# Third attention layer's finishing laid into the units of the expert mixture, with split weights streamed from DRAM

## The reference

```python
# L0_gnn, one layer (three in a row); y = attention over 100000 edges and the node itself
y = gat_conv(h, src, dst, w_l[i], a_s[i], a_d[i], b_l[i])
y = jax.nn.elu(y)
y = layer_norm(y, g_l[i], bt_l[i])
h = y + identity
...
x = x + _L0_gnn_ref(xn, ...) + _L0_mix_ref(xn[None], ...)[0]
x = x + _L0_ffn_ref(_layernorm(x, axis=-1)[None], ...)[0]

# L0_ffn: 8 experts, all computed for every node
w = jax.nn.softmax(feat @ Wr + br, axis=-1)
h = jax.nn.relu(_bn(jnp.einsum('bfd,edh->bfeh', x, W1) + b1, g1, be1, m1, v1))
h = jax.nn.relu(_bn(jnp.einsum('bfeh,ehk->bfek', h, W2) + b2, g2, be2, m2, v2))
y = jnp.einsum('bfeh,ehd->bfed', h, Wo) + bo
return jnp.einsum('bfed,fe->bfd', y, w)
```

## Time and profile before

| | us |
|---|---|
| median of 3 runs | 6968.39 |
| lowest, highest | 6960.25, 6972.53 |
| the profiled execution's own time | 6968.1 |
| its span in the trace | 6966.3 |
| busy in it: PE, DVE, ACT, POOL | 5315.0, 4790.6, 4135.7, 3522.9 |

### The profile page before, as it was taken

How to read it: one execution, slowest core, us unless ns; L and a number is a source line. 1 busy time by engine, 2 the same in 40 slices (tenths; PEclk the granted TensorE clock), 3 DMA queues, 4 the chain that set the end, 5 groups by cost and what they waited for, 6 DMA issues and landing times. The chain is left out here.

```text
span 6966.3 us, 97579 instructions
## 1 busy us (share of the span) xinstructions
PE 5315.0 (76%) x22260; PEld 3745.2 (54%) x22260; DVE 4790.6 (69%) x13210; ACT 4135.7 (59%) x13375; POOL 3522.9 (51%) x3571
## 2 busy tenths in 40 slices
PE   1768888745888886558888825999998887788698
PEld 1634444433555554535555514888884566565446
DVE  5756666684777777767777786666662487777693
ACT  4568989874989997669999862333335322111142
POOL 3377777727777773577777700000000477777501
PEclk8878888876999998779999867999998998788799
DMA  6344444434444443354444432000007534333402
GB/s 179 121 128 120 120 119 121 115 119 140 122 127 123 124 124 103 122 151 122 127 123 123 121 101 74 18 18 18 27 9 242 195 116 125 108 108 102 131 23 75
DMA packets 483830, 763.81 MB, mean 110 GB/s; under 512 B 85339, under 2 KB 360491, under 8 KB 483307
## 3 DMA queue, kind: packets, MB, share of 16 engines
q0 software_dynamic: 166320, 446.82, 23.1%
q1 hardware_dynamic: 317131, 313.36, 14.2%
HBM read 622.82 MB, written 146.27 MB: 110 GB/s over the span
## 5 line engine op out<-in xcount | busy, mean ns | idle before, releaser
L1810 POOL DMA_INDIRECT gm_got<-scratch_feat,keep_src_tab x2490 | 2378.5, 955 | 798.9 <-issue 657.2
L2032 ACT ACTIVATE gm_got<-gm_got 128x64 f32<-128x64 f32 x9804 | 2387.3, 335 | 6.5 <-DVE gm_got L1946 5.3
L2087 PE MATMUL gm_bank<-gm_got,gm_onehot 128*128 128x264 f32 x4980 | 1790.3, 457 | 493.9 <-DVE gat_acc L1970 290.3
L2087 PEld LDWEIGHTS gm_bank<-gm_got,gm_onehot 128*128 128x128 f32 x4980 | 884.6, 211 | 1112.7 <-ACT gm_got L2032 694.2
L1970 DVE TENSOR_TENSOR gat_acc<-gat_acc,gm_bank 128x264 f32 x2490 | 1057.8, 425 | 512.5 <-PE gm_bank L2087 232.5
L1114 POOL DMA_INDIRECT mix1a_got<-scratch_rel_feat,layer_rel_tab x240 | 238.1, 992 | 1536.5 <-issue 1534.7
L1114 POOL DMA_INDIRECT mix1b_got<-scratch_rel_feat,layer_rel_tab x590 | 591.3, 1002 | 192.9 <-issue 188.7
L1977 DVE TENSOR_TENSOR gm_onehot<-gm_iota,keep_dst_tab 128x640 f32<-128x640 f32 x498 | 405.7, 815 | 201.2 <-PE gm_bank L2087 198.8
L1171 PE MATMUL mix1b_m_bank<-mix1b_got,mix1b_onehot 128*128 128x256 f32 x1180 | 382.7, 460 | 150.7 <-DVE layer_acc L1145 121.5
L837 POOL DMA_INDIRECT scratch_first<-gat_scores,keep_first_pos x150 | 220.5, 1470 | 490.6 <-DVE gat_scores L820 449.2
L1171 PEld LDWEIGHTS mix1b_m_bank<-mix1b_got,mix1b_onehot 128*128 128x128 f32 x1180 | 244.5, 225 | 257.4 <-DVE mix1b_onehot L1123 146.9
(11 more groups left out here) (559 smaller groups left out, 10490.9 us busy)
## 6 DMA issues: line engine op xcount, KB each, us to landing
scratch_rel_feat<-rel_out SPq DMA_DIRECT2D x50, 1024.0 KB, 6.3
gm_got<-scratch_feat,keep_src_tab POOLq DMA_INDIRECT x2490
gm_flags<-scratch_flags SPq DMA_DIRECT2D x84, 300.0 KB
gf_feat<-scratch_feat SPq DMA_DIRECT2D x75, 256.0 KB, 4.0
gf_old<-scratch_hidden SPq DMA_DIRECT2D x75, 256.0 KB, 5.0
scratch_hidden<-gf_h SPq DMA_DIRECT2D x75, 256.0 KB, 4.3
scratch_feat<-gf_row SPq DMA_DIRECT2D x50, 260.0 KB, 3.6
gm_x<-scratch_x SPq DMA_DIRECT2D x50, 256.0 KB
```

Source lines behind the costliest of these rows:

```text
L1810: nc.gpsimd.indirect_dma_start(out=got[:, place // GROUPS, place % GROUPS * GROUP + j, 0:GAT_ROW], out_offset=None, in_=dram["feat"][layer ...
L2032: last = nc.scalar.activation(rows, rows, ACT.Copy, scale=got[:, b, i, D + h:D + h + 1])
L2087: nc.tensor.matmul(bank[i % BANKS][:, 0:GAT_SUM], onehot[:, i % HOTS, :], got[:, v[1] % B, i, :], start=True, stop=True).then_inc(s_sum, 1)
```

## The change

`gat_finish` is only called for the first two layers. For the third, `finish_and_mixture` does its work inside the mixture: `acc` is kept until the stage ends, and the finishing of the next unit's four tiles is part of the front that lies in the steps of this unit. The hidden rows of the third layer are no longer written to DRAM and read back. Since the accumulator takes the room, the weights don't stay in SBUF: a piece is one expert's high and low part of one of the three matrices (512 KB), there are two slots for each matrix, and SP loads a piece as soon as PE has ended the product that used its slot, in every unit again. The split is made once, beside layer 0: each of 24 windows loads one expert's matrix (256 KB), splits it on DVE at slots 12 and 15, and stores 512 KB in the new tensor `ffn_cut`. The loop of units runs five times over two, and three units follow it.

```diff
     DVE_AT = {0: "stats", 4: "add", 2: "aggr", 9: "scale", 12: "high", 15: "low", 19: "neg", 24: "phi"}
...
         if tags in ("first", "both"):
             sp.wait_ge(self.s_xn, it[0] * 2 + after)
             sp.dma_start(self.x[:, :, :], ...).then_inc(self.s_x, 16)
+            sp.wait_ge(self.s_cut, 2 * after)
+            sp.dma_start(self.cuts[after - 1], self.cut[...].bitcast(F32)).then_inc(self.s_cut_sent, 16)
+            if after < len(self.raws):
+                sp.dma_start(self.raw[:, :, :], self.raws[after]).then_inc(self.s_raw, 16)
...
+        elif name == "high" and tags in ("first", "both"):
+            dve.wait_ge(self.s_raw, 16 * n)
+            if n > 1:
+                dve.wait_ge(self.s_cut_sent, 16 * (n - 1))
+            nc.vector.tensor_copy(self.cut[:, 0], self.raw[:, :, :]).then_inc(self.s_cut, 1)
+        elif name == "low" and tags in ("first", "both"):
+            dve.wait_ge(self.s_cut, 2 * n - 1)
+            nc.vector.tensor_tensor(self.cut[:, 1], self.raw[:, :, :], self.cut[:, 0].bitcast(F32), ALU.subtract).then_inc(self.s_cut, 1)
...
# finish_and_mixture, SP
+                for u in range(N_U):
+                    for e in range(E + 2):
+                        for j, s_l in enumerate((s_l1, s_l2, s_l3)):
+                            k = e - j
+                            if 0 <= k < E and u * E + k + 2 < N_U * E:
+                                sp.wait_ge(s_l, u * E + k + 1)
+                                load_weight(j, k + 2)
+                        if e == 2 and u > 0:
+                            store(u - 1)
+                            if u + 1 < N_U:
+                                load_x(u + 1)
+                        if e == 3 and u + 2 < N_U:
+                            sp.wait_ge(s_feat_free, u + 2)
+                            load_feat(u + 2)
+                        if e == 5 and u + 2 < N_U:
+                            sp.wait_ge(s_old_free, u + 2)
+                            load_old(u + 2)
...
# DVE, the unit's steps; ACT's below
-                        if e == 2 and next_loaded is not None:
-                            front_start(1 - s, next_loaded)
-                        if e == 3 and next_loaded is not None:
-                            front_statistics(1 - s)
-                        if e == 5 and next_loaded is not None:
-                            front_end(n + 1, 1 - s)
+                        if after:
+                            if e == 0:
+                                edge_part(n + 1, tile, after)
+                            elif e == 1:
+                                own_part(n + 1, after)
+                            elif e == 3:
+                                elu_norm(n + 1, after)
+                            elif e == 4:
+                                add_rows(n + 1, 1 - s, loaded, after)
+                            elif e == 5:
+                                front_statistics(1 - s, after)
+                            elif e == 6:
+                                front_end(n + 1, 1 - s, after)
...
                     for e in range(E + 1):
+                        if after and e == 4:
+                            root(n + 1, after)
+                        if after and e == 6:
+                            front_root(n + 1, after)
                         if e < E:
                             layer(0, m + (e + 1), e, size)
...
                         if e >= 1:
                             layer(1, m + e, e - 1, size)
-                        if e == 4 and not last:
-                            front_root(n + 1)
+                        if after and e == 0:
+                            scale_own(n + 1, tile, after)
+                        if after and e == 2:
+                            elu(n + 1, after)
...
# PE, ahead of each of the three products of a step
+                    def weight_here(j, e):
+                        pe.wait_ge(s_wj[j][e % 2], m * 8 + (e // 2 + 1) * 16)
...
-        expert_mixture(nc, io, dram, keep)
...
-        gat_finish(nc, io, dram, keep, gathers, layer, scores, acc, layer == GAT_LAYERS - 1)
+        if layer < GAT_LAYERS - 1:
+            gat_finish(nc, io, dram, keep, gathers, layer, scores, acc)
+        else:
+            finish_and_mixture(nc, io, dram, keep, scores, acc)
```

More of the change, by code:

```diff
@@ L2111, in _, with gat_finish @@
                 program(pe, softmax_part, sum_step, PE_AT, side.pe)
-def gat_finish(nc, io, dram, keep, gathers, layer, scores, acc, last_layer):
+def gat_finish(nc, io, dram, keep, gathers, layer, scores, acc):
     H = GAT_HEADS
@@ L3128, in _ @@
-                store(k + 3, 0, last, 16 * (k // 2 + 2), REST)
+                for e in range(2):
+                    for j in range(3):
+                        load_weight(j, e)
+                load_x(1)
+                sp.wait_ge(s_feat_free, 1)
+                load_feat(1)
+                sp.wait_ge(s_old_free, 1)
+                load_old(1)
+                for u in range(N_U):
[15 more added lines that the diff above has]
+                            load_old(u + 2)
@@ L3130, in _ @@
+                store(N_U - 1)
             @block.vector
@@ L3156, in front_statistics @@
+                def front_statistics(s, size):
+                    for i in range(size):
                         last = nc.vector.bn_stats(stats[:, i, :], x[:, s, i, :])
@@ L3291, in layer, with unit @@
                     last.then_inc((s_h1, s_h2)[j], 1)
-                def unit(n, s, m, last, size=QUAD):
+                def unit(n, s, m, tile, size=QUAD, after=QUAD):
                     act.wait_ge(s_logit, n)
```

347 lines of the change are left out of this document (211 added, 136 removed).

## The result

| | before | after |
|---|---|---|
| median of 4 runs, us | 6967.6 | 6854.83 |
| lowest, highest | 6960.25, 6972.53 | 6846.57, 6867.2 |
| ratio (95% interval) | | 0.9841 (0.9829 to 0.9854) |
| the profiled execution | 6968.1 | 6867.2 |

The change is 113 us faster by the medians, 101 by the two profiled executions (that of after is the slowest of its four). The forecast was 100 us, 6868.

What follows compares the result with a forecast made beforehand. Layer 3's finishing ran alone on DVE, then TensorE bounded the mixture, busy 76.14 of 80 us. From the profiled 6968.1: -167 start, +60 units, +7 layer 0 gave 6868 us, range 6815 to 6920.

Steps and rivals of the forecast that it cites:

- The start, -167: From the border after layer 2 to the mixture's first wide matmul: 202.2 us replaced by a short start of 35.2.
- The walk: One mixture unit timed step by step from its first route matmul: new TensorE waits of 3.8 us a unit.
- step 5: Mixture unit: DVE's split of expert 5 ends just when wanted, no slack; TensorE waits 0.95 us for expert 3's gather.
- step 6: Mixture unit: ACT's root goes ahead of its layer, which ends late; TensorE waits 0.9 us.
- step 7: Mixture unit: DVE's normalised rows come at 65.3, transposes could start at 63.4; TensorE waits 1.9 us.
- +60: Twelve mixture units: 5.0 us each from waits 3.8, hand-overs 0.4 and low clock 0.8; ends +30 and +96.
- The weights' stream at 0: Mixture units: weight pieces reloaded from DRAM, landing in about 4 us against 13.9 available, costed at 0.
- Layer 0, +7 within 0 and 28: Layer 0: DVE's split, 1.2 us in each of 24 windows, mostly hidden; +7 us, bounds 0 and +28.
- (a): Rival, mixture units: covers hold and a unit stays at 77.4 us; 6808 in all; chance 0.13.
- (b): Rival, mixture units: low clock in every unit and hand-overs make waits 8 to 9 us a unit; 6910; chance 0.15.
- (d): Rival, mixture units: the weights' stream sets the pace, slower than before below 163 GB/s; chance 0.04.
- (c): Rival, layer 0: DVE's split or POOL's standing still paid in full, +28 instead of +7; 6889; chance 0.08.

Runs made afterwards that it cites:

- e6: Changed kernel with the finishing left out of the units, done only at the start for the first unit; weights still streamed: 6817.68 us.
- e9: Changed kernel, finishing spread over one step more, turn a step later, ACT's roots behind the first layer of steps 4 and 7: 6824.37 us, ratio to before 0.9795.
- e7: Changed kernel with both roots on ACT behind the first layer of their step instead of ahead: 6831.25 us, ratio to before 0.9809.
- e8: Changed kernel with DVE's thirteen units written out, other engines keeping their loop: 6834.77 us, ratio to before 0.9816.
- e5: Changed kernel with every reload of a weight piece followed by a second such load into spare buffers: 6887.28 us, against 6966.29 before.
- e4: Changed kernel with weights loaded once and no reloads in the units: 7980.28 us, against 8097.65 before in that slower set.
- e1: Changed kernel with the cast of layer 0's split left out, subtraction kept: 7959.40 us, in the set where before took 8097.65.
- e2: Changed kernel with the subtraction of layer 0's split left out, cast kept: 7996.48 us, in the set where before took 8097.65.
- e11: e9 with DVE's units written out and the turn behind its step's third product: 7903.43 us against 8085.89 before, ratio 0.9773.
- e10: e9 with DVE's units written out and layer 0's split at slots 26 and 28: 6828.34 us, ratio to before 0.9798.
- e3: Changed kernel with layer 0's cast and subtraction at slots 26 and 28 instead of 12 and 15: 7940.31 us, ratio to before 0.9804.

## Why the prediction was right, and where it wasn't

**The start, -167: right.** 166.8, and 35.4 us where the sum of small operations has 35.2 (its terms as they stand add up to 34.8).

**The places of the new waits: right; the fourth not named.** The walk names step 5 for DVE's gather, step 6 for ACT's layer behind the root, step 7 for the rows, and all three are in the rows of after. e6 shows that they come with the finishing, e9 and e7 that they come of its distribution over the steps and of the roots' place: DVE does the same 756 us there. That is 10.0 us a unit more than before, where the walk had 11.8 with hand-overs. The walk's claim that step 5 has no slack for the split holds too (0.27). What it has not is the loop's return, which e8 shows.

**Their size, +60: too high.** The walk's 3.8 and 0.4 for hand-overs were 3.3 in the unit that was read, the half clock's 0.8 was 0.4: (37.7 - 28.2)/2/12. The term that was mis-sized is the clock and the hand-overs taken on top. Over twelve units 11 times 3.3 is 36 (the last front is of two tiles and costs nothing), the loop's return adds 5.8 in waits, the clock 4.8: 47, measured 45.3. That the total came within 1 us of the forecast in the profiled execution is luck in part: +60 was 15 too high, layer 0 and what lies behind the mixture 14 too low. The median was 13 us below the forecast.

**The weights' stream at 0: right for the waits**, by e6 and the rows of after; e5 shows room for almost twice the traffic. Whether it has a part in the half clock, up to 0.6 us a unit by e4, is open. Only in the last unit of two tiles, where a step is half as long, it costs 2.1 us, which the sum had not.

**Layer 0, +7 within 0 and 28: 11.7**, and 8.3 to 11.5 in e5 to e9 with the same program there. The size was near, the reason wasn't. The prediction took a small value since "DVE waits 2.20 us for TensorE about where the split goes", so it priced DVE's time alone. Of the 11.7, 4.6 are longer gathers, which no idle time of DVE hides. The other 7 are idle time of POOL, and their cause stays open. That TensorE comes later because the cast stands ahead of the one-hot matrix is not borne out. Its waits for that matrix in layer 0, before and after:

```profile
PEld gm_bank L2087 <- DVE gm_onehot L1977: 9.0, 4, 2.5
PE gm_bank L2087 <- DVE gm_onehot L1977: 2.1, 1, 2.1
```

```profile
PEld gm_bank L2108 <- DVE gm_onehot L1998: 9.0, 4, 2.5
PE gm_bank L2108 <- DVE gm_onehot L1998: 2.1, 1, 2.1
```

They are the same, and its waits for DVE's accumulation are 114.8 and 113.1 us. Those for the rows that ACT scales are longer (PE 81.9 for 74.6, PEld 288.5 for 284.5), which would fit rows that were gathered late; that was not tested.

The prediction cited the Trainium skill (SBUF — State Buffer, § Who interferes with whom) for the cast as the one that stops POOL; e1 and e2 show that, at these slots, the cast does little and the subtraction much. The same section of the Trainium skill has a rule that fits this, which was not applied: a DVE operation with two inputs in SBUF is in the way of a GpSimd instruction that reads SBUF. The traces agree with it on both sides. The subtraction has both inputs in SBUF and holds the gathers; the one-hot operation of 0.82 us has one of its two in PSUM, and before the change the 145 gathers that began while it ran, or up to 0.4 us ahead of it, took 0.95 us on the mean, 1.07 at most. That POOL's gather reads its offsets at its start was not shown apart.

**The rivals.** (a), periods of 77.4, came about only with the finishing left out (77.6, e6) or re-laid with the turn in the gap (75.9, e11); its condition, slack in step 5, was missing. (b) and (d) did not come. (c) came by a fifth: 11.7 between 7 and 28.

## What to carry to other kernels

A stage's free time on an engine is worth what its fullest steps leave: the same 120 us of DVE work cost 45 us when laid into steps that overran by 2, and 16 when it was spread over a step more with the roots behind a layer (e9). With DVE's units written out and the transposes put where TensorE waited in any case (e11) nothing of it was left to see. An operation that waits for another engine goes behind, not ahead of, what its own engine owes to the bound engine. And when work is added to a loop, look at the first operation behind its return.

## What was not expected of the hardware

- The return of a long loop on DVE: 3.2 to 3.4 us with nothing to wait for, at each of four returns; none with the units written out, 0.6 to 0.7 when the loop's body was a fifth shorter (before, e6). With twice the DMA traffic (e5) it was 3.9 to 4.1. What passes in that time no row shows.
- TensorE's clock can weigh as much as the waits and doesn't follow them simply. In e8 half clock fell from 37.7 us to 20.9 with 5.8 us less waiting, in e11 to 11.0 with 40 less; but from e9 to e10, 4.8 us less waiting came with 40.8 us in place of 34.0. After a wait of 2.9 or 2.3 us the granted clock was at 1.2 GHz for 3.4 us in some units and not in others of the same kernel; in e11, with the wait at 1.4, two of twelve units show any half clock.
- A subtraction with both inputs in SBUF, begun 0.07 us ahead of a gather on POOL, lengthened it from 0.95 to 1.43 us; begun 0.24 us behind its start (after, 649.72 and 649.48), to 1.74:

```profile
649.48 1.74 POOL L1831 DMA_INDIRECT gm_got<-scratch_feat,keep_src_tab  x1 [0.30 <-issue]
649.72 0.67 DVE L1285 TENSOR_TENSOR gm_cut<-gm_raw,gm_cut 128x512 fp32r<-128x512 f32 x1
```

In both the gather ends some 0.83 us behind the subtraction (544.84 and 544.01, 651.22 and 650.39), and so it does for all 23 subtractions of e1 that began from 0.08 us ahead of a gather's start to 0.32 behind it. One begun 0.37 us behind the start left the gather at 0.95. Where both began nearly together (e3 and e10, 0.04 us ahead to 0.06 behind), one of the two gave way: in nine cases the gather took 1.47 us, in twelve it took 0.94 to 0.96 and the subtraction up to 0.76.

- A cast of 0.42 us (e2, e4 and after) held a gather at two places. Begun 0.06 to 0.10 us ahead of it, it made it 1.14 to 1.18 us, with its end some 0.82 us behind the cast's; begun 0.44 to 0.59 us behind its start, 0.98 to 1.13 us, with its end 0.12 us behind the cast's. Begun in between, as most were, or from 0.70 us on, it left it at 0.95. That is why the casts cost little here.
